# A fused transformer block: the order of tiles one to three written anew, the loop over the other tiles unchanged

## What is computed

```python
x = x + attn(layernorm(x))
x = x + ffn(layernorm(x))

def attn(h):            # per row: 32 heads of 32
    q = (h @ wq.T + bq).reshape(B, S, H, D)
    k = (h @ wk.T + bk).reshape(B, S, H, D)
    v = (h @ wv.T + bv).reshape(B, S, H, D)
    scores = einsum('bshd,bstd->bsht', q, k) / sqrt(D)
    probs = softmax(scores, axis=-1)
    return einsum('bsht,bstd->bshd', probs, v).reshape(B, S, E)

def ffn(h):             # 8 experts, 2 taken per row, rank 16
    logits = einsum('bsd,ed->bse', h, gate_w)
    w_full = scatter(softmax(top_k(logits, 2)))
    base = einsum('bsd,od->bso', h, base_w) + base_b
    low = einsum('bsd,erd->ebsr', h, lora_A)
    return base + 2.0 * einsum('ebsr,eor,bse->bso', low, lora_B, w_full)
```

## Time and profile before

| what | value |
|---|---|
| median of 3 runs | 1276.71 us (1274.11 to 1278.17) |
| the profiled execution's own time | 1278.39 us |
| its span in the profile | 1275.3 us |
| TensorE busy | 97% of the span |
| VectorE, ScalarE, GpSimd busy | 84%, 58%, 33% |
| TensorE's share of the chain that ended last | 84% |
| one tile in the loop (194.99 to 232.30 us) | 37.31 us |

### The profile page before, as it was taken

The page is one execution under the profiler, slowest core; times in us unless marked ns, Lnnn a source line. Parts: engine busy times, 40 slices in busy tenths (PEclk is TensorE's granted clock), DMA queues, the critical chain, the costliest instruction groups (busy, mean ns, idle before and its releaser), DMA issues.

```text
span 1275.3 us, 30571 instructions
## 1 busy us (share of the span) xinstructions
PE 1242.0 (97%) x12314; PEld 642.1 (50%) x12314; DVE 1067.5 (84%) x1492; ACT 743.3 (58%) x1149; POOL 426.5 (33%) x340
## 2 busy tenths in 40 slices
PE   6899989999999999999999999999999999999998
PEld 4554445455554545455454555545455555545454
DVE  5799898888888888888888888888888888888886
ACT  4876646665556666555666655566665556666431
POOL 0113433334423333442333344233334423333320
PEclk9999999999999999999999999999999999999999
DMA  9823543344444334444433444443344444333330
GB/s 367 295 67 85 133 100 92 89 101 115 101 96 97 96 84 101 115 101 97 97 96 84 102 115 101 97 96 96 84 103 115 99 98 96 96 84 87 85 84 33
DMA packets 295447, 136.41 MB, mean 107 GB/s; under 512 B 265072, under 2 KB 266096, under 8 KB 295408
## 3 DMA queue, kind: packets, MB, share of 16 engines
q1 hardware_dynamic: 228688, 112.28, 33.6%
q10 hardware_dynamic: 66720, 23.60, 7.8%
HBM read 86.03 MB, written 33.03 MB: 93 GB/s over the span
## 4 chain that ended last, share of the span: by engine, by line
PE 84%; DVE 7%; DMA 3%; issue 2%; ACT 2%; SPq 1%; POOL 0%; DVEq 0%; ACTq 0%
PE acc L1630 23%; PE dense_acc L1790 23%; PE acc L1639 22%; PE attn_ps L1732 7%; PE dense_acc L1800 2%; DMA work<-wT_dram 2%; PE low_ps L1769 1%; PE low_ps L1762 1%; PE low_ps L1763 1%; PE dense_acc L1805 1%; DMA turn_dram<-x_turned 1%; DVE w_lo_k L1059 1%; ACT work L401 1%; DVE work L1196 1%; DVE work L1157 1%
## 5 line engine op out<-in xcount | busy, mean ns | idle before, releaser
L1790 PE MATMUL dense_acc<-base_parts,x 128*128 128x512 f16 x1488 | 331.2, 380 | 1.1 <-issue 1.0
L401 ACT COPY work<-work 32x512 f16<-32x512 f16 x498 | 306.5, 615 | 12.4 <-PE attn_ps L1732 0.3
L1790 PEld LDWEIGHTS dense_acc<-base_parts,x 128*128 128x128 f16 x1488 | 145.7, 99 | 165.6 <-issue 2.2
L632 POOL TENSOR_TENSOR work<-work 128x1024 f16<-128x1024 f32 x32 | 68.4, 2137 | 225.9 <-ACT work L917 225.9
L1196 DVE SCALAR_TENSOR_TENSOR work<-acc,acc_to_a,biases_sb 128x512 f32<-128x512 f32 x192 | 136.3, 738 | 1.8
L582 POOL TENSOR_TENSOR columns<-columns 128x1 f32<-128x1 f32 x31 | 9.1, 293 | 362.9 <-ACT work L797 362.9
L763 ACT CAST x_hi<-x_turned 128x1024 f16<-128x1024 f32 x31 | 32.4, 1044 | 155.3 <-PE acc L1639 154.4
L1630 PE MATMUL acc<-w_hi_k,x_hi 128*128 128x512 f16 x496 | 117.5, 380 | 1.6 <-issue 1.6
L1630 PE MATMUL acc<-v_parts,x_hi 128*128 128x512 f16 x496 | 117.5, 380 | 0.0
L1639 PE MATMUL acc<-w_hi_k,x_lo 128*128 128x512 f16 x496 | 117.2, 379 | 0.0
L1630 PE MATMUL acc<-w_hi_q,x_hi 128*128 128x512 f16 x496 | 117.2, 379 | 0.0
(11 more groups left out here) (217 smaller groups left out, 2070.1 us busy)
## 6 DMA issues: line engine op xcount, KB each, us to landing
work<-x_dram SPq DMA_DIRECT2D x64, 512.0 KB, 3.6
work<-work SPq DMA_DIRECT2D x256, 64.0 KB, 2.0
work<-x_dram SPq DMA_DIRECT2D x124, 128.0 KB, 3.8
out_dram<-work SPq DMA_DIRECT2D x31, 512.0 KB, 2.6
x_turned<-turn_dram ACTq DMA_DIRECT2D x30, 512.0 KB, 3.3
work<-wT_dram SPq DMA_DIRECT2D x16, 512.0 KB, 9.9
turn_dram<-x_turned SPq DMA_DIRECT2D x64, 128.0 KB, 3.9
turn_dram<-x_turned ACTq DMA_DIRECT2D x60, 128.0 KB, 4.4
```

What stands on the lines that cost most here:

```text
L401: copy(diag[c * QD:(c + 1) * QD, :, c, j::NQ, :], src).then_inc(vdiag_ready, 1)
L632: nc.gpsimd.tensor_tensor(v_parts_t[:, :, 1, :], turned3, v_parts_t[:, :, 0, :], ALU.subtract).then_inc(v_lo_ready, 1)
L1790: nc.tensor.matmul(dense_acc[n][:, :], rows_part[:, k, :], w_part[:, k, cols], start=(k == 0 and m == 0), stop=False)
```

## The change

Nothing is computed in another way, and the loop body is the same. The order in steps 1 and 2 of ScalarE, VectorE and GpSimd is new:

- `keys(t)` on TensorE no longer waits for the low part of its rows before its first matmul, but ahead of the first matmul that reads the low part (this one holds for every tile). `spread_stats(4)` stands behind the last piece of `dense_first`.
- In step 2 `base_bias(0)` on GpSimd stands ahead of `x2_low(1)`. The low part of tile 4's rows (`x1_low(4)`) is made by GpSimd, not by VectorE.
- `fetch_x2(1)` is issued by SyncE's queue, not by ScalarE's. In step 2 `fetch_x2(2)` is issued behind `v_high(3)`, and `park_x2(2)` behind the normalising of tile 5.
- VectorE takes two more of the 16 spread copies of tile 2 from ScalarE; ScalarE takes one group of tile 1 in two parts around `probabilities_high(1)`.
- On VectorE `gate_top(0)`, `gate_rest(0)` and the last chunks of the base weight stand ahead of `stats2(1)`; in step 2 `gate_top(1)` and `gate_rest(1)` stand ahead of `norm2(2)`. Evictions of tile 2's keys stand side by side.

```diff
--- before.py
+++ after.py
@@ -552,6 +552,8 @@
                     load_bias("base")
                 if t + 1 < T:
                     park_x2(sp, t, (0, 1))
+                if t == 1:
+                    fetch_x2(sp, 1)
 
             store(T - 2)
             for n in range(NB):
@@ -676,13 +678,15 @@
 
             def step(t):
 
-                x2_low(t - 1)
                 if isinstance(t, int) and t == 2:
                     base_bias(0)
+                x2_low(t - 1)
                 if tile(t, 1):
                     base_bias(t - 1)
                 if tile(t, 3):
                     row_root(t + 3)
+                if isinstance(t, int) and t == 2:
+                    x1_low(4)
                 if tile(t, 1):
                     root(t, var_ready2, rstd_ready2)
                     second_lo(t + 1)
@@ -876,24 +880,24 @@
                 exponentials(1)
                 spread(1, (0, 1))
                 copy_quad_stats(3)
+                spread_v(nc.scalar.copy, 2, range(NQ - 1))
                 probabilities_high(1)
-                spread(1, (2,))
+                spread_v(nc.scalar.copy, 2, range(NQ - 1, NQ))
                 k_high(2)
                 x2_high(0)
+                high_parts("base", w_hi["base"], 5, 6)
                 scale_quads(3)
-                high_parts("base", w_hi["base"], 5, 6)
+                high_parts("base", w_hi["base"], 6, 7)
                 x1_high(3)
-                high_parts("base", w_hi["base"], 6, 7)
                 q_high(2)
+                high_parts("base", w_hi["base"], 7, KC)
+                gate_exp(0)
                 row_statistics(4)
-                gate_exp(0)
-                high_parts("base", w_hi["base"], 7, KC)
+                low_copy(0)
                 copy_quad_stats(4)
-                low_copy(0)
                 scale_quads(4)
                 park_x2(act, 1, (2, 3))
                 v_high(2)
-                fetch_x2(act, 1)
 
             def k_high(t):
 
@@ -956,7 +960,7 @@
                     x2_high(t - 1)
                     spread(t, (1,))
                     probabilities_high(t)
-                    spread(t, (2,))
+                    spread_v(nc.scalar.copy, 2, range(NQ // 2))
                 else:
                     x2_high(t - 1)
                     spread(t, (0,))
@@ -970,6 +974,14 @@
                 if tile(t, 2):
                     x1_high(t + 2)
                 q_high(t + 1)
+                if isinstance(t, int) and t == 2:
+                    gate_exp(1)
+                    normalise_quads(5)
+                    park_x2(act, 2, (2, 3))
+                    low_copy(1)
+                    v_high(3)
+                    fetch_x2(act, 2)
+                    return
                 park_x2(act, t, (2, 3))
                 gate_exp(t - 1)
                 if tile(t, 3):
@@ -1495,32 +1507,32 @@
 
                 dve.wait_ge(vt_ready, 2)
                 add_bias(2, 0, FIRST, 0, a_acc, a_biased)
+                add_bias(2, 1, FIRST, 1, a_acc, a_biased)
                 sum_exponentials(1)
                 probabilities(1)
-                add_bias(2, 1, FIRST, 1, a_acc, a_biased)
+                spread_v(nc.vector.tensor_copy, NQ - 1)
                 turn_first(2)
-                spread_v(nc.vector.tensor_copy, NQ - 1)
 
                 dve.wait_ge(at_ready, 3)
                 add_bias(2, 0, SECOND, 2, b_acc, b_biased)
                 add_bias(2, 1, SECOND, 0, b_acc, b_biased)
                 base_split(4, 5)
                 turn_context(1)
+                base_split(5, 6)
                 turn_quads(3)
-                base_split(5, 6)
                 turn_second(2)
+                base_split(6, 7)
+                gate_top(0)
                 attention_end(1)
-                stats2(1)
-                gate_top(0)
-                base_split(6, 7)
                 gate_rest(0)
                 base_split(7, KC)
+                stats2(1)
+                low_low(0)
                 norm2(1)
                 turn_x2(1)
 
                 dve.wait_ge(bt_ready, 3)
                 add_bias(2, 0, "v", 1, v_acc, v_biased)
-                low_low(0)
                 add_bias(2, 1, "v", 2, v_acc, v_biased)
                 turn_third(2)
 
@@ -1533,13 +1545,32 @@
                 dve.wait_ge(vt_ready, 3)
                 add_bias(3, 0, FIRST, 0, a_acc, a_biased)
                 add_bias(3, 1, FIRST, 1, a_acc, a_biased)
+                spread_v(nc.vector.tensor_copy, 2, range(NQ // 2, NQ))
                 spread_v(nc.vector.tensor_copy, NQ - 1)
                 probabilities_low(2)
+                turn_quads(4)
                 finish(0, 0)
                 finish(0, 1)
-                turn_quads(4)
                 turn_first(3)
-                attend_step(2)
+
+                dve.wait_ge(at_ready, 4)
+                add_bias(3, 0, SECOND, 2, b_acc, b_biased)
+                add_bias(3, 1, SECOND, 0, b_acc, b_biased)
+                turn_context(2)
+                first_low(3)
+                attention_end(2)
+                turn_second(3)
+                stats2(2)
+                gate_top(1)
+                gate_rest(1)
+                norm2(2)
+                turn_x2(2)
+
+                dve.wait_ge(bt_ready, 4)
+                add_bias(3, 0, "v", 1, v_acc, v_biased)
+                low_low(1)
+                add_bias(3, 1, "v", 2, v_acc, v_biased)
+                turn_third(3)
 
             def step(t):
                 if isinstance(t, int) and t == 2:
@@ -1620,7 +1651,7 @@
 
             any_low = [None, None]
 
-            def project(g, n, bank, done):
+            def project(g, n, bank, done, low_tile=None):
 
                 i = 1 if g == "v" else 0
 
@@ -1635,6 +1666,9 @@
                 with pe.If(any_low[i] > 0):
                     for k in range(KC):
                         nc.tensor.matmul(dst, x_hi[:, k, :], w_lo[g][:, k, cols], start=False, stop=False)
+                if low_tile is not None:
+
+                    pe.wait_ge(xlo_ready, low_tile + 1)
                 for k in range(KC):
                     mm = nc.tensor.matmul(dst, x_lo[:, k, :], w_hi[g][:, k, cols], start=False, stop=(k == KC - 1))
                 mm.then_inc(done, 1)
@@ -1841,11 +1875,11 @@
                 pe.wait_ge(w_lo_done["base"], KC - 1)
                 for n in range(NB):
                     dense(n, KC - 2, KC - 1)
-                spread_stats(4)
                 turn_low(0)
                 pe.wait_ge(w_lo_done["base"], KC)
                 for n in range(NB):
                     dense(n, KC - 1, KC)
+                spread_stats(4)
 
             def context(p):
 
@@ -1916,10 +1950,9 @@
             def keys(t):
 
                 pe.wait_ge(xhi_ready, t + 1)
-                pe.wait_ge(xlo_ready, t + 1)
 
                 pe.wait_ge(b_biased, 2 * t)
-                project(FIRST, 0, 0, a_acc)
+                project(FIRST, 0, 0, a_acc, t)
 
                 pe.wait_ge(v_biased, 2 * t - 1)
                 project(FIRST, 1, 1, a_acc)
```

## The result

| | before | changed |
|---|---|---|
| median of 8 runs each | 1276.65 us (1274.11 to 1278.64) | 1281.54 us (1280.29 to 1283.17) |
| the profiled execution's own time | 1278.39 us | 1282.01 us |
| its span | 1275.3 us | 1279.6 us |

The ratio is 1.0039, with a 95% interval of 1.0028 to 1.0050: the change costs 0.4%, some 5 us, where 2.1 us were forecast. The time lies inside the range of the forecast; slower by more than 0.3% had a chance of 0.24.

What follows compares the result with a forecast made beforehand. TensorE's own order was taken to bound the kernel, with waits in steps 1 and 2. +0.2 at `queries(4)` plus 1.9 for the slow clock made +2.1 us: median 1276.71 to 1278.8 us, range 1275.0 to 1282.5.

Steps and rivals of the forecast that it cites:

- `keys(2)`: Step 1, TensorE: with the wait for the low rows moved behind the high half, 1.57 us gained.
- the dense pieces: Step 1, TensorE: `base_split(5, 6)` now ahead of `turn_quads(3)`, so most of the 0.96 us wait at `dense_first` goes.
- `spread_stats(4)`: Step 1: tile 4's statistics at 150.6, TensorE waits about 3.5 us, `scores(2)` starts about 152.0 against 149.84.
- As before, nothing follows: Step 1: the sum counted no slow clock behind the gap of some 3.5 us at `spread_stats(4)`.
- the slower rival: Slow clock at the `spread_stats(4)` gap delays `shift(2)`, +1.4 us, later fetch +1.1: +4.6 in all, 1281.3 us; chance 0.26.
- Only 0.4 late: Step 2: with `fetch_x2(1)` on SyncE, tile 2's exponentials start near 156.0, against 155.60 before.
- From the sum of exponentials to `turn_x2(2)`: Step 2, VectorE: `x1_low(4)` leaves, -1.21 us; gate comes in, +2.5; `norm2(2)` may shrink by 0 to 1.7.
- The gate's early place: Step 2: `low_ready(1)` near 183, so the 2.43 us wait and slow clock go; `scores(3)` 3.9 us ahead.
- The fetch: Step 3: tile 2's rows are fetched through DRAM near 193.8, +1.9 us; bounds +0.9 to +3.0.
- The collision with `base_bias(2)`: Step 3: `probabilities(3)` no longer meets this GpSimd addition, 1.2 us for 2.92: -1.7; bounds -1.7 to 0.
- `queries(4)`: Step 3, second half: TensorE there at 203.0, goes on at 207.1; 3.9 us become a 4.1 us wait, +0.2.
- The clock behind it: Step 3: slow clock behind the 4.1 us wait at `queries(4)` costs 1.9 us; bounds 0 to 3.9.

Runs made afterwards that it cites:

- `rows_ahead_of_gate`: Changed kernel with `norm2(2)` and `turn_x2(2)` ahead of `gate_top(1)` and `gate_rest(1)` on VectorE; 1280.41 us, ratio 1.0013.
- all three: Changed kernel with `norm2(2)`, `turn_x2(2)` ahead of the gate, ScalarE's parking ahead of gate and tile 5's scalings, `fetch_x2(2)` on SyncE; 1279.10 us, ratio 1.0009.

## Why the prediction was right or wrong

- **`keys(2)`: right; the dense pieces: not.** The wait ahead of `keys(2)` is gone. But of its 1.57 us half came back as 0.79 at `context(1)`, for `probabilities_low(1)` on GpSimd. And the 0.96 at `dense_first`, of which most was to go, turned into 0.62 at `turn_low(0)` and 0.87 at the last base chunk. Neither cost anything, since TensorE then stood at `spread_stats(4)`.
- **`spread_stats(4)`: right in mechanism and size.** Forecast 3.5 us of wait, statistics at 150.6 and `scores(2)` 2 us worse; measured 2.96, 151.26 (150.41 without the late start) and 2.43. `row_root(4)` had indeed been queued behind `root(1)`: swapping the two takes all of it away.
- **"As before, nothing follows": wrong, and the slower rival right.** I gave 0.26 to a slow clock at that gap. It came in every run that had the gap: the matmuls of `scores(2)` or those just ahead of them were slow. And `shift(2)` waited 1.13 us for them, as the rival had it. "Only 0.4 late" for VectorE in step 2 measured 1.99 at the sum of exponentials; the rival's +1.4 on top of it was 1.6.
- **From the sum of exponentials to `turn_x2(2)`: 0.5 us more, forecast 0.1 less.** `norm2(2)` shrank from 2.53 to 0.80, as hoped, and a cast of 128x8 in the gate grew from 0.17 to 2.03, beside `second_lo(3)` on GpSimd. The collision had not gone but changed its victim. Two more terms, each of 1.4 us, are not in the sum and cancel: the spread copies, six now, took 1.94 us where four had taken 3.36, and `first_low(3)` took 2.79 us instead of 1.38, beside `base_bias(1)` on GpSimd. That is luck. I had forecast 0 to +1.7 for `turn_x2(2)`; it was +2.51.
- **The gate's early place: right.** 2.43 us and the slow clock behind it are gone. `scores(3)` is 2.32 us ahead, forecast 3.9. The difference lies at `spread_stats(5)`, 2.02 us later than before and not 0.5: `row_statistics(5)`, which it needs, waited 2.54 us for a load. Taking the gap away brings `scores(3)` to 3.26 ahead, so the gap is part of that; the rest stays open.
- **The fetch: size within its bounds, cause wrong in part.** +2.58 in a range of +0.9 to +3.0, where the sum had +1.9. I put it down to ScalarE's four scalings, and by two ways, the landing and ScalarE's queue, came to one number. The runs show `turn_x2(2)`, 2.51 late, and the wait for tile 5's quads instead of the scalings. Of the two ways the landing holds the fetch in the changed kernel, the queue in `rows_ahead_of_gate`, where the landing was short. A term was missing altogether: +1.0 from the fetch's issue to `x2_high(2)`.
- **The collision with `base_bias(2)`: right.** -1.70, as forecast.
- **`queries(4)`: wait right, sum too low.** 3.76 and 4.61 against 4.1, but TensorE goes on 1.52 and 2.28 us later than before, not 0.2. **This is the step that failed:** +0.2 for "the 3.9 turn into 4.1" rested on an eviction at 206.3, and that came at 208.50, or 207.65 without this execution's late start. Of these 1.3 us the fetch has 0.7 and the way from the fetch to `x2_high(2)` 1.0, less 0.4 that came back beyond the forecast.
- **The clock behind it, +1.9: right in size, in the first profile by luck.** There it did not fall, and 1.96 us were lost all the same, most of it by the collision of `x1_low(5)` with `second_lo(4)`, which was not in the sum. In the second profile it fell and cost 1.69 us, and that collision stayed away.

In all +3.48 and +3.97 at `scores(4)` for a forecast of +2.1, and +4.9 in the medians. The second timing of the changed kernel gave a ratio of 1.0032, some 4.1 us, so the 0.9 to 1.4 between profiles and medians is not clear of noise. The likeliest case, a change within 0.3%, did not come. The rival for slower, at +4.6, describes what happened better than the forecast did, and my 0.26 for it was too little: I had one wait of 2.43 us with a slow clock behind it in the rows, and a forecast wait of 3.5 us in the sum.

## What to carry to other kernels

A gain won in one tile is kept only if everything that the next tile needs is early too: follow the longest round trip (here rows through DRAM: two parkings, a landing of mostly 5 us, a fetch of 3.3 to 5.2) before moving work ahead of its first instruction. An instruction that waits for a load holds what is issued behind it in its queue, DMAs included, even if its own work is short. Where two holders end together, taking away one shows little: the fetch moved by 0.6 and 0.5 us with one edit each, and by 1.4 with all three. And a loss of the forecast size is no proof of the forecast cause: here a collision on VectorE cost what the slow clock was to cost.
